# A fused attention and mixture-of-experts kernel on one Trainium2 core: where the shared expert's down weights are prepared

## What is computed

```python
def reference(x, ctx_1024, mask_Bx1xSxS2_if1, g_xattn, g_ffn, ...):
    x = x + tanh(g_xattn[0]) * xattn(layernorm(x), ctx_1024, ctx_1024, mask, w_q, b_q, ..., w_o, b_o)
    x = x + tanh(g_ffn[0]) * ffn(layernorm(x), gate_w, eg, eu, ed, sg, su, sd)

def ffn(xf, ...):
    scores = softmax(xf @ gate_w.T)
    topk_w, topk_idx = top_k(scores, 2)          # normalised to a sum of one
    y = sum over the two experts e of w_e * (silu(xf @ eg[e].T) * (xf @ eu[e].T)) @ ed[e].T
    y = y + silu(xf @ sg.T) * (xf @ su.T) @ sd.T
```

## Time and profile before

| what | value |
|---|---|
| median of three runs | 873.52 us |
| the profiled execution's own time | 871.96 us |
| its span, first to last instruction | 870.2 us |
| PE busy | 838.1 us (96%) |
| weight loads of PE busy | 734.8 us (84%) |
| DVE busy | 595.1 us (68%) |
| ACT busy | 522.5 us (60%) |
| POOL busy | 462.0 us (53%) |
| mean granted PE clock | 0.993 |
| PE's share of the chain that ended last | 82% |

### The profile page before, as it was taken

The page is one execution under the profiler, slowest core; times in us unless marked ns, Lnnn a source line. Parts: engine busy times, 40 slices in busy tenths (PEclk is TensorE's granted clock), DMA queues, the critical chain, the costliest instruction groups (busy, mean ns, idle before and its releaser), DMA issues.

```text
span 870.2 us, 19205 instructions
## 1 busy us (share of the span) xinstructions
PE 838.1 (96%) x6183; PEld 734.8 (84%) x6184; DVE 595.1 (68%) x1225; ACT 522.5 (60%) x1846; POOL 462.0 (53%) x551
## 2 busy tenths in 40 slices
PE   8788999999999999999999999999999999999995
PEld 7566788888888889999988888888888888889994
DVE  5899899999988667976565666655665665444442
ACT  3999999998999535646555544445445445323221
POOL 5688667587575443666641444444444424364442
PEclk9899999999999999999999999999999999999998
DMA  7124223322221232323351444443334432232221
GB/s 221 41 80 143 95 75 109 90 82 91 73 85 63 79 105 70 112 97 109 103 154 38 76 75 70 70 66 66 65 67 69 73 49 38 31 55 36 36 42 19
DMA packets 104762, 67.85 MB, mean 78 GB/s; under 512 B 63514, under 2 KB 93055, under 8 KB 104671
## 3 DMA queue, kind: packets, MB, share of 16 engines
q1 hardware_dynamic: 90743, 48.93, 19.9%
q0 software_dynamic: 12864, 17.57, 12.2%
q10 hardware_dynamic: 1064, 0.21, 0.1%
HBM read 34.78 MB, written 25.82 MB: 70 GB/s over the span
## 4 chain that ended last, share of the span: by engine, by line
PE 82%; ACT 5%; DVE 5%; issue 4%; POOL 2%; DMA 1%; DVEq 0%; SPq 0%; ACTq 0%; POOLq 0%
PE p_s L680 23%; PE p_f L697 12%; PE p_f L2843 8%; PE p_s L347 6%; PE p_f L2888 4%; ACT prob L1551 4%; PE p_s L2843 4%; PE p_t L2773 3%; PE p_s L2754 3%; PE p_t L358 3%; PE p_m L2800 3%; PE p_m L2735 2%; PE p_m L2788 2%; PE p_s L2888 2%; PE p_s L2946 1%
## 5 line engine op out<-in xcount | busy, mean ns | idle before, releaser
L1551 ACT ACTIVATE prob<-p_s,negmax 128x77 f32<-128x77 f32 x512 | 161.6, 375 | 7.1 <-DVE negmax L2099 7.0
L1551 ACT ACTIVATION_READ_ACCUMULATOR prob<-p_s,negmax 128x1 f32 x512 | 129.7, 257 | 0.0
L537 POOL DMA_INDIRECT big_xin<-xn_scratch,slot_id x52 | 52.2, 1003 | 125.9 <-DMA big_placed<-big_xin 103.2
L581 ACT ACTIVATE big_sil<-p_s 128x512 f32<-128x512 f32 (+1 forms) x78 | 46.5, 596 | 115.7 <-PE p_s L680 100.5
L545 POOL DMA_INDIRECT out_rows<-big_yout,slot_id x52 | 85.2, 1639 | 55.4 <-DVE big_yout L643 38.6
L680 PE MATMUL p_s<-big_fxT_hi,big_w_hi 128*128 128x512 f32 (+1 forms) x286 | 112.8, 395 | 0.3 <-ACT big_w_hi L573 0.3
L680 PE MATMUL p_s<-big_fxT_lo,big_w_hi 128*128 128x512 f32 (+1 forms) x286 | 112.9, 395 | 0.0
L680 PE MATMUL p_s<-big_fxT_hi,big_w_lo 128*128 128x512 f32 (+1 forms) x286 | 112.2, 392 | 0.0
L1174 POOL TENSOR_TENSOR prob<-prob,rinv 128x616 f32<-128x616 f32 x64 | 78.6, 1238 | 61.7 <-DVE rinv L2106 61.7
L626 DVE TENSOR_TENSOR big_hid<-p_s,big_sil 128x512 f32<-128x512 f32 (+1 forms) x78 | 53.9, 691 | 76.3 <-ACT big_sil L581 70.5
L697 PE MATMUL p_f<-wd_hi,big_hT_hi 128*128 (+1 forms) x312 | 85.5, 280 | 0.0
(11 more groups left out here) (347 smaller groups left out, 2541.9 us busy)
## 6 DMA issues: line engine op xcount, KB each, us to landing
big_placed<-big_xin SPq DMA_DIRECT2D x176, 32.0 KB
xr<-in_x SPq DMA_DIRECT2D x16, 256.0 KB, 2.8
x_scratch<-xr SPq DMA_DIRECT2D x16, 256.0 KB, 2.5
xn_scratch<-xn SPq DMA_DIRECT2D x16, 256.0 KB, 2.1
xt_scratch<-xnT SPq DMA_DIRECT2D x16, 256.0 KB, 2.7
xin<-xt_scratch SPq DMA_DIRECT2D x16, 256.0 KB, 3.8
x1in<-x_scratch SPq DMA_DIRECT2D x16, 256.0 KB, 3.1
out_rows<-syout SPq DMA_DIRECT2D x16, 256.0 KB, 2.2
```

The costliest lines, as they stand in the source:

```text
L537: pool.indirect_dma_start(xin[:, t, :], None, v["xn_d"], bass.IndirectOffsetOnAxis(slot_id[:, column(j, t)], 0)).then_inc(s_rows, 16)
L1551: last = act.activation(prob[n % 2][t][:, m * PW + h * SK:m * PW + (h + 1) * SK], p_s[:, 2 * t + h // 4, col:col + SK], ACT.Exp, bias=negm ...
```

## The change

Groups 8, 9 and 10 leave the units 2 and 3 of `first_steps` on PE, ACT and DVE and go into the first pair of steps, i = 4 and 5. All three use bank p_f[0] there, one after the other. Group 8's transposes wait for the first product of the shared unit (s_hid), which frees p_f[0]. PE's first gate and up chunk waits for 8 groups, the fourth for all 11. The loads of the first two expert matrices on SP go from step 4 to step 6.

```diff
+        def w_bank(w):
+            return p_f[w % 2] if w < 8 else p_f[0]
...
                 if i == FIRST:
                     load_rows(1)
+                if i == FIRST + 2:
                     expert_matrix(0)
                     expert_matrix(1)
...
             def w_hi(w):
...
-                bank = p_f[w % 2]
+                bank = w_bank(w)
...
                 t_copy(1, 3)
-                w_hi(8)
                 xn_copy(0)
...
                 t_copy(2, 0)
-                w_hi(9)
                 exps(3, 0, HH // 2)
...
                 t_copy(2, 3)
-                w_hi(10)
                 xn_hi(0)
...
                     t_copy(i - 1, 2)
+                if n == 0:
+                    w_hi(8)
                 if has(i):
                     exps(i, 1, HH // 2)
...
                     exps(i, 2)
+                if n == 0:
+                    w_hi(9)
+                if has(i):
                     exps(i, 3)
...
                     t_copy(i - 1, 0)
+                if n == 0:
+                    w_hi(10)
...
                 w_lo(7)
-                w_lo(8)
                 half_max(2, 3)
...
-                w_lo(9)
                 last_t_copy(2)
-                w_lo(10)
...
                     q_lo(i + 1)
+                if n == 0:
+                    w_lo(8)
                 if has(i):
                     half_max(i, 2)
...
                     recip(i, 2)
+                if n == 0:
+                    w_lo(9)
...
                     half_max(i, 1)
+                if n == 0:
+                    w_lo(10)
                 if has(i - 2):
                     attended(i - 2)
...
                     if n == 0:
-                        pe.wait_ge(s_wlo, PER)
+                        pe.wait_ge(s_wlo, 8)
                         pe.wait_ge(s_wpad, 4)
...
                 elif c == 3:
                     wait(pe, s_y, n)
+                    if n == 0:
+                        pe.wait_ge(s_wlo, PER)
...
                 if w < 2:
                     pe.wait_ge(s_vall, 2)
+                elif w < 8:
+                    pe.wait_ge(s_wlo, w - 1)
+                elif w == 8:
+                    pe.wait_ge(s_wlo, 8)
+                    pe.wait_ge(s_hid, 1)
                 else:
-                    pe.wait_ge(s_wlo, w - 1)
-                bank = p_f[w % 2]
+                    pe.wait_ge(s_wlo, w)
+                bank = w_bank(w)
...
                 prob_T(1, 3)
-                w_T(8)
                 xn_T(0)
...
                 scores(3, 0)
-                w_T(9)
                 out_proj(1)
...
                 prob_T(2, 1)
-                w_T(10)
                 scores(3, 2)
...
                 if n > 0:
                     down(n - 1, 0)
+                else:
+                    w_T(8)
...
                 if n > 0:
                     down(n - 1, 1)
+                else:
+                    w_T(9)
...
                     scores(i, 0)
+                if n == 0:
+                    w_T(10)
+                if has(i):
                     scores(i, 1)
```

More of the change, by code:

```diff
@@ L2899, in w_T @@
                     pe.wait_ge(s_vall, 2)
-                else:
-                    pe.wait_ge(s_wlo, w - 1)
-                bank = p_f[w % 2]
+                elif w < 8:
[3 more added lines that the diff above has]
+                    pe.wait_ge(s_hid, 1)
+                else:
+                    pe.wait_ge(s_wlo, w)
+                bank = w_bank(w)
                 src_raw = raw["gud".index(kind) % 2]
```

## The result

Twenty executions each on the same chip: the changed kernel has a median of 873.33 us (871.84 to 874.82), the kernel before 872.07 us (869.38 to 874.35, but for one stray execution of 1171.56 us, which the ratio leaves out). The ratio is 1.0015, with a 95% interval of 1.0008 to 1.0022: the change costs 1.3 us, with an interval of 0.7 to 1.9 us. That is within 0.3%, the case that had most of the chance, and 873.33 us lies in the range. The forecast step was +0.6 us. The forecast time, 874.1 us, stood on the three runs of 873.52 us; on the 872.07 us measured beside the changed kernel the same step gives 872.7 us.

The account below looks back on a forecast made before the run. Before 95.31 us the chain of waits alternates between ACT, DVE and PE; from there PE alone bounds. The terms -0.6 + 0.60 + 0.49 + 0.1 gave +0.6 us on the 873.52 us median, so 874.1 us, range 871.9 to 876.0 us.

Parts of the forecast that it names:

- Items 1 and 2: Unit 2, group 8 leaving PE and DVE: 0.22 us gained; 0.6 us of the DVE gain lost again.
- Item 3: Unit 3, group 9's ACT copy removed: exponentials at 67.40 us start about 0.6 us earlier, limited by their row maximum.
- Item 4: Unit 3, group 10 removed: its ACT copy lies in the shadow of PE's xn transposes; nothing gained.
- Item 5: Steps 4 and 5, PE: the three groups' transposes, 0.44 us each, go into holes of 1.23, 0.99 and 0.51 us; no cost.
- Item 6: Step 4, group 8's DVE subtraction ahead of the maximum of unit 4, half 2: +0.60 us; its ACT copy free.
- Item 7: Group 9's ACT copy between unit 4's third and fourth exponentials: +0.49 us; its DVE part free.
- Item 8: Step 5, group 10's DVE piece ahead of the residual update: PE waits about 0.1 us at the fourth gate and up chunk.
- Items 9 and 10: SyncE's load of shared rows goes out 2 us later, cost 0; the shared unit's wait for 8 groups gains nothing.
- A and B: PE stretches: unit 1's fourth probability transposes to step 4's first scores, then to unit 5's second scores; forecast -0.6 and +1.09 us.
- Nothing is given back and step 5 is hit in full: Units 2 and 3 give nothing, group 10's transposes are not hidden: +1.6 us, 875.1 us; chance 0.13.
- The whole chain piece is given back: The removed pieces count in full, the added ones are hidden: -1.5 us, 872.0 us; chance 0.15.
- The clock falls once more: Thinner PE work in units 2 and 3 brings a second clock fall: 1.4 to 2.85 us, 877.0 us at most; chance 0.07.

Follow-up runs that it names:

- the repeat: Both kernels measured once more, unchanged, in one comparison: the kernel before 872.43 us, the changed one 872.93 us (ratio 1.0009).
- with filler: 14 useless matmuls put in PE's early holes of both kernels: the kernel before 870.14 us, the changed one 870.79 us.

## Why the prediction was right, point by point

The forecast was right in sign and case, and in size by the cuts: +0.6 us by its sum, +0.77 us by the cuts in two pairs of profiles, +1.3 us by the first ratio (0.7 to 1.9), +0.8 us by the repeat's ratio (-0.1 to 1.7) and +0.65 us by the medians with filler. The +1.3 us is twice the forecast and at the upper end of its own range (-0.3 to +1.3 us). That the total came so close was in part luck: errors of opposite sign cancelled.

- **Items 1 and 2 (group 8's place: 0.22 us passed on)**: too much, by all of it. PE's own 0.44 us came out, and 0.34 us of idle took its place (57.78 us). The fourth and the fifth probability transposes share the bank p_t, and between them ACT has to empty it. The two are 1.41 us apart before (55.23 to 56.64 us) and after (56.37 to 57.78 us). I had looked for the waits of the instruction behind group 8 on DVE, and not for the next event on PE, which was already due for another reason. That item 2's 0.6 us on DVE would be lost again was right.
- **Item 3 (group 9's ACT copy and what follows)**: the bound was the right one, its move was not. ACT waits for the row maximum, and I had that 0.44 us earlier; it came 0.13 us earlier (11.13 against 11.26 us behind the first cut), since item 1's 0.22 us was not there and the residual update ahead of it moved by 0.13 us only. The item gave 0.32 us. With item 1 it had been put at 0.6. **Item 4 (group 10 gives nothing)**: right (20.90 us).
- **Item 5 (the three PE pieces go into holes)**: right for all three. A slip in it: the piece of DVE at 84.38 us is 0.03 us in the chain; nothing hung on its length.
- **Item 6 (group 8 on DVE, +0.60)**: mis-sized, 0.38 to 0.41 us. The chain of waits named DVE there, and DVE was the engine. But 0.19 us of the piece between 87.54 and 88.51 us was a wait that the added work filled. The sum of durations, 0.78 us, against the distance of the starts, 0.97 us, shows it; I had not made that comparison.
- **Item 7 (group 9 on ACT, +0.49)**: 0.51 us, right.
- **Item 8 (group 10 on DVE, about 0.1)**: the place was right, and it measured 0.2 us. PE's transposes of unit 6 come 4.97 us after the second scores of unit 5 (97.03 to 102.00 us), where it was 4.78 us before. The fourth chunk starts 0.09 us late, which is the 0.1 us of the sum, and its second matmul comes 0.23 us behind its first, not 0.12, which makes the other 0.1 us. From there to the transposes of unit 6 PE keeps its 0.12 us, so the residual update, my "edge", cost nothing.
- **Items 9 and 10 (SyncE, and the wait for 8 groups)**: no effect was seen behind 112 us, and in the kernel with only group 10 moved, which has the moved loads, A and B stayed at 20.90 and 19.19 us. I did not test them alone.

So A's gain was put 0.3 us too high, B's cost 0.2 us too high and C's 0.1 us too low, and most of that cancels. By the cuts step 4 starts 0.32 us earlier, just short of the 0.4 to 0.8 us that I had named, and unit 5's second scores 0.58 us later, inside the 0.3 to 0.7 us. The misses in A and B have one cause: I priced a piece of the chain by its length, or by one neighbour's wait, without asking what else already held the next start. Here, where engines come within 0.3 us of each other, both a removed and an added piece were worth less than that. One of the signs of being wrong, a second stretch at 0.50 of the clock, did show in the first profile; it was a poor sign, since the kernel before has it too.

**The rivals.** *Nothing is given back and step 5 is hit in full*: half of it was true (group 8 gave nothing), but group 9's place gave 0.32 us and group 10's transposes were hidden. *The whole chain piece is given back*: no, 0.32 of 1.53 us. *The clock falls once more*: a second fall was in the profile, with nearly the size that I had named (0.7 to 2.0 us against 1.4 to 2.85), but it stands ahead of the change and comes by chance in both kernels. In the units that the change thins no profile without filler has a fall. My bound on what the fall at 28.4 us costs, 2.85 us, was far off: 0.7 us at most, because PE filled its holes first. It also began a little before 28.4 us: the window ahead has 0.96, not the 1.00 that I had given to all other rows.

## What to carry to other kernels

Moving a piece is worth the distance between the starts of its neighbours on the engine that bounds, with and without it, and not the piece's duration. Before a piece of the chain is counted, look for the next event on the same engine, and ask whether another wait (here a shared PSUM bank) already holds it there. When two kernels differ by less than a fall of the clock costs, cut both traces at starts outside the falls and compare the stretches; the spans of single profiles mislead. When several transfers share one bank, a late place for one of them holds up the next on all engines.

## What the hardware showed that I had not expected

- The granted clock of the same kernel differs from execution to execution: 0.988 to 0.994 in 84 executions. A fall between 39 and 46 us came in five of the eight profiles without filler, and costs 0.7 to 2.0 us. Which kernel gets it is chance: the changed one had it once in two profiles, and so had the kernel before. In the longest, it began at 39.0 us, in a hole of 1.08 us on PE and behind one of 0.45 us. What decides it is open.
- Useless work on PE in its early holes makes this kernel 0.21% to 0.26% faster in three measurements, with 14 matmuls or 28 transposes. In all five profiles with filler the clock is 1.00 from 23 to 60 us.
- A fall in unit 3 (72 us, a product of 1.93 us taking 3.27 to 3.34 us) came in two of the three profiles of the filled kernel before, and in none without filler. I don't know why, and three profiles are too few to say that it isn't chance.
